# Four banks for the turned rows and two for the logits at the end of the attention layers a1 and a2

## The chip, the cores and the metric

The kernel runs on one core of one Trainium2 chip. The metric is the device time of one execution in microseconds. Three runs of the kernel before were timed, and their median is the number that the change is measured by. Beside them one execution was profiled; all rows below come from it.

## The reference

The reference is a stack of four pairs of layers over x, of 8 batches x 256 tokens x 256 features, with a context of 77 keys per batch:

```python
x = x + tanh(g_xattn[n]) * Ln_xattn(_layernorm(x), ctx, ...)   # n = 0..3
x = x + tanh(g_ffn[n])   * Ln_ffn(_layernorm(x), ...)
```

Attention has 16 heads, of width 16 in layers 0 and 3 and of width 64 in layers 1 and 2. Layer 1 normalises queries and keys to unit length and its output once more by a layer norm; layer 2 has a mask. The expert layers begin with a router. What matters here is the start of each expert layer: `_layernorm(x)`, and from it the router's logits, `xn @ Wr + br` (8 columns in layer 1; in layer 2 8 columns for the gate and 96 for the low-rank parts, 104 in all).

## The kernel before, in words

The kernel is one program of eight stages, a0 f0 a1 f1 a2 f2 a3 f3 (a: attention, f: expert layer). Between stages all engines meet at a barrier, and the semaphores are cleared. x, `residual` in the trace, stays in SBUF as 16 tiles of 128 tokens, two tiles to a batch.

Each attention stage is written by `attend` (line 2278). Its work is placed by hand on steps s; each engine goes through the same steps in order, and functions such as `scores_at(s)` and `output_at(s)` say which piece falls on which step. PSUM has 8 banks: banks 0 to 3 take scores, 4 and 5 the turned probabilities, 6 and 7 are spare. All other uses (queries, squares, values, output, and what is described next) go through the two spare banks in turn: `uses` lists them in TensorE's order, `place` numbers them, `spare` gives bank 6 or 7 by the number's parity, and `take_spare` makes TensorE wait until the use two places earlier has been emptied.

The front (`front_part`, line 807) is the start of the following expert layer, and is done within the attention stage. For each batch b:

- `variance(b)` on VectorE (lines 889 to 894): statistics of x after the attention's output has been added
- `power(b)` on GpSimd (L898): the inverse root
- `normalise(b)` on VectorE (L907): two tiles of x into `xn`. In a2 `xn` is a ring of two batches, so that `normalise(b)` waits for turn(b-2); in a1 every batch has its own place (`xn_all`), which the SP queue also stores to HBM
- `add_row(b)` on GpSimd (L920), in a2 only: a row added to x after `normalise(b)`
- `turn(b)` on TensorE (L927): 4 transposes of 128x128 into one bank
- `turned_out(b)` on ScalarE (L933): the bank to `xT`
- `route(b)` on TensorE (L943): `xT` times the router's weights
- `logits_out(b)` on VectorE (L955, and in a2 L958 too): logits (and low-rank parts) out of the bank

In a1 and a2 (`small` is false, it means heads of width 16) the turns stand at the very end: `rows_at(s)` gives batch b at step GROUPS + 2 + b, when scores, values and the last `output` product have been issued. `route` follows one step behind the turn, and `logits_out` one more. On TensorE a step is `turn(b)`, then `route(b-1)`. On VectorE it is, where they fall on the step, `add_output`, `variance`, `normalise`, `logits_out`, in this order. In a2 `normalise(b+2)` falls on the step of `turn(b)` (batches 2 to 7). In a1, where the output is normalised once more (`own`), `variance(7)` falls on the step of turn(3), and `normalise(7)` on that of turn(4); `variance(7)` waits for GpSimd's additions of batch 7 (L2728).

Of the kernel before, what the change touches and what calls it, by code (L numbers as in the profile page):

```python
# [35 lines left out]
GROUPS = HEADS // GROUP  # L36
# [2241 lines left out]
def attend(env, scope, n, t, front):  # L2278
# [3 lines left out]
    nc, dram, psum, x, ident, tg = env["nc"], env["dram"], env["psum"], env["x"], env["ident"], env["tg"]  # L2282
# [3 lines left out]
    small = hd == 16  # L2286
# [5 lines left out]
    GROUPS = NBATCH * STEPS  # L2292
# [45 lines left out]
    if mask == "given":  # L2338
        mask8, mask_cap = sb("mask8", [P, TILES, CTX], U8), sb("mask_cap", [P, TILES, CTX])
        loads += [(mask8[:], dram["mask"])]  # L2340
    sems = {k: env["sem"](f"{name}l_{k}") for k in (
        "loaded", "made", "q_ready", "q_out", "q_done", "sq_ready", "sq_copied", "sq_turned", "sq_out", "q_inverted",
        "scored", "s_free", "chain", "shift", "exped", "probs", "turned", "pt_out", "multiplied", "att_out",
        "y_ready", "y_out", "inv_spread", "inv_out", "topped", "row_added", "gated_row", "wo_in", "stats", "var_done", "rstd_done", "applied", "gained", "added")}
# [11 lines left out]
    def queries_at(s):  # L2356
        b, j = divmod(s + Q_AHEAD, STEPS)
        return (b, j) if b < NBATCH and j < NQ else None

    def squares_at(s):  # L2360
        h = (s + 4) // 2
        return h if own and s % 2 == 0 and 0 <= h < 2 * NBATCH else None

    def scores_at(s):
        return s + 2 if 0 <= s + 2 < GROUPS else None

    def norm_at(s):
        return s + 1 if 0 <= s + 1 < GROUPS else None

    def turn_at(s):  # L2370
        return s if 0 <= s < GROUPS else None

    def values_at(s):
        return s // 2 - 1 if s % 2 == 0 and 0 <= s // 2 - 1 < 2 * NBATCH else None

    def output_at(s):
        return (s - 5) // STEPS if s >= 5 and (s - 5) % STEPS == 0 and (s - 5) // STEPS < NBATCH else None
# [10 lines left out]
    def rows_at(s):  # L2388
        if small:
            return output_at(s - 3)  # L2390
        return s - BEHIND if 0 <= s - BEHIND < NBATCH else None

    def logits_at(s):
        if small:
            return output_at(s - 4)
        return rows_at(s - 1)

    def logits_out_at(s):
        if small:
            return output_at(s - 5)  # L2400
        return rows_at(s - 2)


    uses = []
    for s in range(FIRST, LAST):
        if queries_at(s):
            uses.append(("q", queries_at(s)[0] * NQ + queries_at(s)[1]))
        if squares_at(s) is not None:
            uses += [("square", squares_at(s)), ("square_turned", squares_at(s))]
        if values_at(s) is not None:  # L2410
            uses += [("values", values_at(s) * AV + m) for m in range(AV)]
        if output_at(s) is not None:
            uses.append(("output", output_at(s)))
        if rows_at(s) is not None:
            uses.append(("rows", rows_at(s)))
        if logits_at(s) is not None:
            uses.append(("logits", logits_at(s)))
    place = {use: k for k, use in enumerate(uses)}
    left_by = {"q": sems["q_out"], "square": sems["sq_copied"], "square_turned": sems["sq_out"], "values": sems["att_out"],
# [2 lines left out]
    def spare(kind, k):  # L2422
        return psum[:, 6 + place[kind, k] % 2, :]

    def take_spare(pe, kind, k):
        before = place[kind, k] - 2
        if before >= 0:
            pe.wait_ge(left_by[uses[before][0]], uses[before][1] + 1)
        return spare(kind, k)

    def score_banks(g):
        return psum[:, 2 * (g % 2):2 * (g % 2) + 2, 0:4 * keys].rearrange("p b (h k) -> p b h k", k=keys)


    scores_read = "exped" if own else "s_free" if mask else "shift"
# [5 lines left out]
    with nc.Block() as block:  # L2441
# [9 lines left out]
        def _(pe):  # L2451
# [28 lines left out]
            def scores(g):  # L2480
                b, hf, tile = group(g)
                rows = slice(tile * P, (tile + 1) * P)
                if rope:
                    pe.wait_ge(sems["q_done"], b + 1)
                else:
                    pe.wait_ge(sems["q_out"], b * NQ + min(NQ, (hf + 1) * max(1, NQ // 2)))
                if g >= 2:
                    pe.wait_ge(sems[scores_read], g - 1)
                if small:
                    for j in range(2):  # L2490
                        part = slice(64 * j, 64 * j + 64)
                        last = nc.tensor.matmul(psum[:, 2 * (g % 2) + j, 0:4 * keys], qT[b % 2][part, hf, rows],
                                                keysT[part, hf, b, :, :], start=True, stop=True)
                else:
                    for j in range(CH):
                        c = hf * CH + j
                        for odd in range(2):
                            part = slice(hd * odd, hd * odd + hd)
                            last = nc.tensor.matmul(psum[:, 2 * (g % 2) + odd, j * keys:(j + 1) * keys],
                                                    qT[b % 2][part, c, rows], keysT[part, c, b, :],  # L2500
                                                    start=True, stop=True)
                last.then_inc(sems["scored"], 1)
# [51 lines left out]
            for s in range(FIRST, LAST):  # L2554
                if scores_at(s) is not None:
                    scores(scores_at(s))
                if queries_at(s):
                    queries(*queries_at(s))
                if turn_at(s) is not None:
                    turn(s, 0)  # L2560
                if squares_at(s) is not None:
                    squares(squares_at(s))
                if turn_at(s) is not None:
                    turn(s, 1)
                if squares_at(s) is not None:
                    turn_squares(squares_at(s))
                if values_at(s) is not None:
                    for m in range(AV):
                        weigh_values(values_at(s), m)
                if output_at(s) is not None:  # L2570
                    output(output_at(s))
                if rows_at(s) is not None:
                    front["turn"](pe, rows_at(s), take_spare(pe, "rows", rows_at(s)))
                if logits_at(s) is not None:
                    front["route"](pe, logits_at(s), take_spare(pe, "logits", logits_at(s)))

        @block.scalar
        def _(act):
# [71 lines left out]
            for s in range(FIRST, LAST):  # L2650
                if queries_at(s):
                    queries_out(*queries_at(s))
                if squares_at(s) is not None:
                    squares_out(squares_at(s))
                if turn_at(s) is not None:
                    turned_out(s)
                if values_at(s) is not None:
                    for m in range(AV):
                        values_out(values_at(s), m)
                if scores_at(s) is not None:  # L2660
                    exps(scores_at(s))
                if rows_at(s) is not None:
                    front["turned_out"](act, rows_at(s), spare("rows", rows_at(s)))

        def add_row(pool, b):
            where = slice(b * TPB, (b + 1) * TPB)
# [88 lines left out]
        def _(dve):  # L2755
# [116 lines left out]
            for s in range(FIRST, LAST + 1):  # L2872
                if output_at(s - 1) is not None:
                    add_output(output_at(s - 1))
                if scores_at(s) is not None:
                    soft(scores_at(s))
                if norm_at(s) is not None:
                    norm(norm_at(s))
                if own and output_at(s - 2) is not None:
                    apply_norm(output_at(s - 2))  # L2880
                if output_at(s - 1 - LAG) is not None:
                    b = output_at(s - 1 - LAG)
                    dve.wait_ge(sems["added" if own else "y_out"], b + 1)
                    front["variance"](dve, b)
                if normed_at(s) is not None:
                    front["normalise"](dve, normed_at(s))
                if logits_out_at(s) is not None:
                    front["logits_out"](dve, logits_out_at(s), spare("logits", logits_out_at(s)))
                if values_at(s) is not None and small:
                    values_out(values_at(s))  # L2890
                if squares_at(s) is not None:
                    sum_squares(squares_at(s))
                if rope and queries_at(s) and queries_at(s)[1] == NQ - 1:
                    turn_positions(queries_at(s)[0])
# [120 lines left out]
```

## Time and profile before

| | us |
|---|---|
| median of 3 runs | 1899.26 |
| lowest and highest | 1893.53, 1905.22 |
| the profiled execution | 1904.71 |
| its span, first to last instruction | 1902.9 |
| mean granted clock of TensorE | 0.945 of full |

In the rows, PE is TensorE, DVE is VectorE, ACT is ScalarE, POOL is GpSimd, and L927 is line 927. Times count from the start of the span. The granted clock is given as a share of 2.4 GHz: 1.00 is that, and 0.50 is 1.2 GHz.

### The profile page before, as it was taken

The page shows a single profiled execution, that of the slowest core. Times are in us where ns is not written, and L with a number is a line of the kernel's source. Part 1 is how long each engine was busy: PE and PEld are TensorE (multiplying, and loading weights), DVE is VectorE, ACT ScalarE, POOL GpSimd, SP SyncE. Part 2 cuts the span into 40 slices and gives each one's busy share as a digit, 9 for nine tenths or more (in the row PEclk, how much of TensorE's full clock was granted, in tenths as well). Part 3 has the DMA queues.
Part 4 walks back from the last instruction along what each step waited for, and adds up shares of the span by engine and source line. Part 5 has one row for each costly group of instructions (what it writes and reads, how often), then busy time and mean ns, then how long its engine had stood idle before and what let it go on. Part 6 is the DMA issues. An engine that isn't in the chain of part 4 may idle for free. (4 is left out here: it accounts for less than half of the span.)

```text
span 1902.9 us, 32108 instructions
## 1 busy us (share of the span) xinstructions
PE 1708.5 (90%) x11648; PEld 1415.0 (74%) x11648; DVE 1266.2 (67%) x2324; ACT 944.4 (50%) x1681; POOL 539.8 (28%) x499
## 2 busy tenths in 40 slices
PE   6998799978899998399999979999789889889997
PEld 4666799943577777399999747888679656678996
DVE  5886687636445563788888658767364678865764
ACT  4653466533676762266666325444254245514660
POOL 2231333241133332244444111000200043403426
PEclk8998899998999997599999989999789999989999
DMA  4002587520100000567777420000010010023864
GB/s 115 12 21 67 190 250 254 154 62 23 52 1 12 7 12 17 193 208 231 230 229 226 161 66 35 1 1 1 1 29 1 12 49 18 18 87 125 255 191 133
DMA packets 96389, 178.41 MB, mean 94 GB/s; under 512 B 25968, under 2 KB 60682, under 8 KB 95162
## 3 DMA queue, kind: packets, MB, share of 16 engines
q1 hardware_dynamic: 84072, 144.23, 23.4%
q0 software_dynamic: 11904, 32.52, 5.9%
q8 instruction: 77, 1.26, 0.3%
q14 instruction: 48, 0.39, 0.1%
q10 hardware_dynamic: 288, 0.00, 0.0%
HBM read 149.70 MB, written 27.00 MB: 93 GB/s over the span
## 5 line engine op out<-in xcount | busy, mean ns | idle before, releaser
L1757 POOL DMA_INDIRECT f_block_rows_home<-normed_x,f_token_of_sb x138 | 169.3, 1227 | 274.3 <-PE psum L1824 229.8
L1804 PE MATMUL psum<-f_block_h_sb,f_w1h_home 128*128 128x256 f32 x736 | 215.1, 292 | 20.2 <-DVE f_w1l_home L1997 9.5
L1804 PE MATMUL psum<-f_block_l_sb,f_w1h_home 128*128 128x256 f32 x736 | 211.0, 287 | 0.0
L1804 PE MATMUL psum<-f_block_h_sb,f_w1l_home 128*128 128x256 f32 x736 | 210.9, 287 | 0.0
L2458 PE MATMUL psum<-a_xT_home,context_w 128*128 128x256 f32 x704 | 180.8, 402 | 16.9 <-PEq L123 13.3
L1814 PE MATMUL psum<-f_w2h_home,f_hidden_h_home 128*128 128x256 f32 x644 | 187.7, 291 | 1.8 <-DVE f_result_sb L1665 0.9
L1814 PE MATMUL psum<-f_w2l_home,f_hidden_h_home 128*128 128x256 f32 x644 | 182.1, 283 | 0.0
L1814 PE MATMUL psum<-f_w2h_home,f_hidden_l_home 128*128 128x256 f32 x644 | 182.0, 283 | 0.0
L2458 PEld LDWEIGHTS psum<-a_xT_home,context_w 128*128 128x128 f32 x704 | 131.3, 196 | 48.0 <-issue 23.1
L2623 ACT ACTIVATE a_probsT_sb<-psum 77x1024 f32<-77x1024 f32 (+1 forms) x128 | 130.8, 1022 | 68.8 <-PE psum L2510 66.2
L1804 PEld LDWEIGHTS psum<-f_block_h_sb,f_w1h_home 128*128 128x128 f32 x736 | 143.9, 195 | 28.3 <-issue 18.4
L1905 ACT ACTIVATE f_hidden_sb<-psum,f_b_sb 128x256 f32<-128x256 f32 x276 | 115.5, 470 | 73.5 <-PE psum L1804 73.3
L2510 PE MATMUL psum<-identity,a_probs_sb 128*77 128x128 f32 (+1 forms) x1024 | 141.5, 280 | 11.0 <-DVE a_inv_sb L2798 8.9
L2510 PEld LDWEIGHTS psum<-identity,a_probs_sb 128*77 128x77 f32 (+1 forms) x1024 | 115.6, 142 | 46.3 <-DVE a_inv_sb L2798 19.7
L2550 PE MATMUL psum<-a_wo_sb,a_attT_sb 128*128 128x256 f32 x640 | 146.8, 385 | 2.6 <-ACT a_attT_sb L2645 1.4
L1804 PEld LDWEIGHTS psum<-f_block_l_sb,f_w1h_home 128*128 128x128 f32 x736 | 144.0, 196 | 0.0
L1804 PEld LDWEIGHTS psum<-f_block_h_sb,f_w1l_home 128*128 128x128 f32 x736 | 143.8, 195 | 0.0
L2550 PEld LDWEIGHTS psum<-a_wo_sb,a_attT_sb 128*128 128x128 f32 x640 | 121.3, 194 | 19.9 <-ACT a_attT_sb L2645 2.7
L1997 DVE TENSOR_TENSOR f_w1l_home<-f_w_sb,f_w1h_home 128x1024 fp32r<-128x1024 f32 x92 | 112.4, 1222 | 29.5 <-ACT f_w1h_home L1926 24.7
L1814 PEld LDWEIGHTS psum<-f_w2h_home,f_hidden_h_home 128*128 128x128 f32 x644 | 123.4, 192 | 2.5 <-DVE f_hidden_l_home L1997 2.5
L1814 PEld LDWEIGHTS psum<-f_w2l_home,f_hidden_h_home 128*128 128x128 f32 x644 | 123.6, 192 | 0.0
L1814 PEld LDWEIGHTS psum<-f_w2h_home,f_hidden_l_home 128*128 128x128 f32 x644 | 123.3, 192 | 0.0
(318 smaller groups left out, 3815.2 us busy)
## 6 DMA issues: line engine op xcount, KB each, us to landing
f_w_sb<-in_f_w SPq DMA_DIRECT2D x161, 512.0 KB, 4.8
sorted_y<-f_result_sb SPq DMA_DIRECT2D x46, 256.0 KB
normed_x<-f_xn_all SPq DMA_DIRECT2D x24, 256.0 KB, 2.1
f_b_row_sb<-in_f_b SPq DMA_DIRECT2D x46, 128.0 KB, 3.6
f_w_sb<-in_f_w SPq DMA_DIRECT2D x23, 256.0 KB, 4.9
f_w_sb<-slots SPq DMA_DIRECT2D x16, 256.0 KB, 6.3
f_block_rows_home<-normed_x,f_token_of_sb POOLq DMA_INDIRECT x138, 4.0
residual<-in_x SPq DMA_DIRECT2D x8, 256.0 KB, 6.3
```

Of the source, the lines that this page charges most:

```text
L1757: nc.gpsimd.indirect_dma_start(block_rows[b % 2][:, h, :], None, xs, bass.IndirectOffsetOnAxis(ap=column, axis=0)).then_inc(sems[f"rows_in ...
L1804: last = nc.tensor.matmul(hid_ps(q)[:, m, :], w, rhs, start=(j == 0), stop=(j == len(parts) - 1))
L1814: last = nc.tensor.matmul(y_ps[h], v, w, start=(begin and j == 0), stop=(end and j == len(parts) - 1))
L1905: nc.scalar.activation(hidden[q][:, m, :], hid_ps(q)[:, m, :], func, bias=bias[:, 0, m:m + 1]).then_inc(sems["hidden_out"], 1)
L1997: nc.vector.tensor_tensor(out[:], whole[:], part[:].bitcast(F32), ALU.subtract).then_inc(sems[sem], 1)
L2458: last = nc.tensor.matmul(bank[:, s * SEQ:(s + 1) * SEQ], w[:, k, c * P:(c + 1) * P], xT[:, k, b * SEQ:(b + 1) * SEQ], start=(k == 0), sto ...
L2510: last = nc.tensor.transpose(psum[0:keys, 4 + part, h * P:(h + 1) * P], probs[g % 2][:, 4 * part + h, :], ident[:])
L2550: last = nc.tensor.matmul(bank[:, tile * D:(tile + 1) * D], attT[:, c, tile * P:(tile + 1) * P], wo[:, c, :], start=(c == 0), stop=(c == N ...
L2623: nc.scalar.activation(probsT[h % 2][:, :, tile * P:(tile + 1) * P].rearrange("p (a h) k -> p a h k", a=2), psum[0:keys, 4:6, :].rearrange ...
```

## The change

Where `small` is false, the turned rows go to the four banks 0 to 3 that the scores have left, in turn, and the logits to the two banks 4 and 5 that the turned probabilities have left. Both leave the list of uses of the spare banks. The first turn waits until all scores have been read, the first route until all turned probabilities have been copied out; from then on each waits for its own bank (four back for rows, two back for logits). `route` now follows two steps behind the turn in place of one, and `logits_out` three in place of two. Where `small` is true (a0 and a3) nothing changes. It applies to a1 and to a2.

```diff
@@ def logits_at / logits_out_at
-        return rows_at(s - 1)
+        return rows_at(s - 2)
...
-        return rows_at(s - 2)
+        return rows_at(s - 3)
@@ uses
-        if rows_at(s) is not None:
+        if small and rows_at(s) is not None:
             uses.append(("rows", rows_at(s)))
-        if logits_at(s) is not None:
+        if small and logits_at(s) is not None:
             uses.append(("logits", logits_at(s)))
@@ new
+    def rows_bank(b):
+        return spare("rows", b) if small else psum[:, b % 4, :]
+
+    def logits_bank(b):
+        return spare("logits", b) if small else psum[:, 4 + b % 2, :]
+
+    def take_rows_bank(pe, b):
+        if small:
+            return take_spare(pe, "rows", b)
+        if b == 0:
+            pe.wait_ge(sems[scores_read], GROUPS)
+        if b >= 4:
+            pe.wait_ge(front["turned_left"], b - 3)
+        return rows_bank(b)
+
+    def take_logits_bank(pe, b):
+        if small:
+            return take_spare(pe, "logits", b)
+        if b == 0:
+            pe.wait_ge(sems["pt_out"], GROUPS)
+        if b >= 2:
+            pe.wait_ge(front["logits_left"], b - 1)
+        return logits_bank(b)
@@ TensorE
-                    front["turn"](pe, rows_at(s), take_spare(pe, "rows", rows_at(s)))
+                    front["turn"](pe, rows_at(s), take_rows_bank(pe, rows_at(s)))
                 if logits_at(s) is not None:
-                    front["route"](pe, logits_at(s), take_spare(pe, "logits", logits_at(s)))
+                    front["route"](pe, logits_at(s), take_logits_bank(pe, logits_at(s)))
@@ ScalarE
-                    front["turned_out"](act, rows_at(s), spare("rows", rows_at(s)))
+                    front["turned_out"](act, rows_at(s), rows_bank(rows_at(s)))
@@ VectorE
-                    front["logits_out"](dve, logits_out_at(s), spare("logits", logits_out_at(s)))
+                    front["logits_out"](dve, logits_out_at(s), logits_bank(logits_out_at(s)))
```

## Rows read from the trace of the kernel before

**Rows 1.** The page's first part: busy time of TensorE, share, instructions.
```profile
PE 1708.5 (90%) x11648; PEld 1415.0 (74%) x11648; DVE 1266.2 (67%) x2324; ACT 944.4 (50%) x1681; POOL 539.8 (28%) x499
```

**Rows 2.** Timeline, TensorE, end of a1: start, length, instruction, count, [idle before <-releaser].
```profile
747.14 1.88 PE L943 MATMUL psum<-f_wr,f_xT_home 128*128 128x8 f32 x8 [1.98 <-DVE f_logits L955]
748.87 1.09 PE L927 MATMUL psum<-identity,f_xn_all 128*128 128x128 f32 x4
749.76 1.71 PE L943 MATMUL psum<-f_wr,f_xT_home 128*128 128x8 f32 x8
...
757.12 3.42 PE L943 MATMUL psum<-f_wr,f_xT_home 128*128 128x8 f32 x16
```

**Rows 3.** Timeline, VectorE, end of a1.
```profile
742.97 0.17 DVE L955 TENSOR_TENSOR f_logits<-psum,f_rb 128x16 f32<-128x16 f32 x1
745.77 0.75 DVE L889 BATCH_NORM_STATS2 stats<-residual 128x6 f32<-128x256 f32 x2 [2.63 <-POOL residual L2728]
...
746.92 0.17 DVE L955 TENSOR_TENSOR f_logits<-psum,f_rb 128x16 f32<-128x16 f32 x1
747.84 0.73 DVE L907 TENSOR_SCALAR f_xn_all<-residual,mv,rstd 128x256 f32<-128x256 f32 x2 [0.75 <-POOL rstd L898]
```

**Rows 4.** Timeline, TensorE, end of a2.
```profile
1341.89 8.64 PE L2550 MATMUL psum<-a_wo_sb,a_attT_sb 128*128 128x256 f32 x32 [0.70 <-ACT a_attT_sb L2645]
...
1351.38 0.66 PE L927 MATMUL psum<-identity,f_xn 128*128 128x128 f32 x4 [0.41 <-DVE residual L2835]
1351.88 1.04 PE L943 MATMUL psum<-f_wr,f_xT_home 128*128 128x104 f32 x8
1353.40 0.63 PE L927 MATMUL psum<-identity,f_xn 128*128 128x128 f32 x4 [0.48 <-DVE f_xn L907]
1357.81 1.38 PE L943 MATMUL psum<-f_wr,f_xT_home 128*128 128x104 f32 x8 [3.78 <-DVE f_low_rank L958]
...
1361.29 2.03 PE L943 MATMUL psum<-f_wr,f_xT_home 128*128 128x104 f32 x8 [1.25 <-DVE f_low_rank L958]
...
1365.42 2.04 PE L943 MATMUL psum<-f_wr,f_xT_home 128*128 128x104 f32 x8 [1.25 <-DVE f_low_rank L958]
...
1372.25 1.92 PE L943 MATMUL psum<-f_wr,f_xT_home 128*128 128x104 f32 x8
...
1374.81 2.34 PE L943 MATMUL psum<-f_wr,f_xT_home 128*128 128x104 f32 x16
```

**Rows 5.** Timeline, VectorE, end of a2 (the second is one tile of the first).
```profile
1352.51 4.89 DVE L907 TENSOR_SCALAR f_xn<-residual,mv,rstd 128x256 f32<-128x256 f32 x6
...
1353.49 1.38 DVE L907 TENSOR_SCALAR f_xn<-residual,mv,rstd 128x256 f32<-128x256 f32 x1
...
1357.33 0.16 DVE L955 TENSOR_TENSOR f_logits<-psum,f_rb 128x16 f32<-128x16 f32 x1
...
1360.15 0.74 DVE L907 TENSOR_SCALAR f_xn<-residual,mv,rstd 128x256 f32<-128x256 f32 x2 [2.40 <-PE psum L927]
...
1377.29 0.35 DVE L958 COPY f_low_rank<-psum 128x192 f32<-128x192 f32 x1
```

**Rows 6.** Timeline, GpSimd, end of a2.
```profile
1353.45 6.30 POOL L920 TENSOR_TENSOR residual<-residual,context_w 128x512 f32<-128x512 f32 x5
```

**Rows 7.** Windows: stretch, length, busy time by engine, granted clock, DMA share, GB/s.
```profile
744.20:760.60 16.40, 14.37 (x69) 13.87 (x68) 2.88 (x14) 2.98 (x5) 2.17 (x3) 0.50 0.05 17
1350.30:1358.50 8.20, 3.52 (x28) 2.83 (x26) 7.08 (x14) 1.79 (x3) 5.82 (x6) 1.00 0.00 0
1358.60:1375.50 16.90, 13.15 (x60) 11.79 (x58) 4.13 (x16) 2.83 (x5) 4.94 (x4) 0.50 0.00 1
1375.70:1379.00 3.30, 1.46 (x13) 1.28 (x12) 1.04 (x5) 0.30 (x1) 0.00 (x0) 1.00 0.00 0
1391.40:1396.10 4.70, 4.70 (x13) 3.72 (x12) 4.09 (x5) 4.28 (x6) 0.00 (x0) 0.50 0.00 0
1396.20:1400.00 3.80, 3.80 (x18) 3.11 (x17) 3.60 (x5) 3.80 (x7) 0.00 (x0) 1.00 0.00 0
```

## The prediction

> **What bounds the kernel now.** I read the page first: TensorE is busy for 90% of the span, no other engine comes near it [rows 1], so what counts is where TensorE stands idle or runs at the lower clock. The change touches only the end of the two attention layers with 64-wide heads: in the code it hangs on `small`, which is false for a1 and for a2 alike, so "second layer" in its name notwithstanding both layers get it. I therefore read two stretches, engine by engine in order of time: 739 to 762 us (end of a1) and 1350 to 1379 us (end of a2). At the end of each stands a barrier of all engines, so whatever ends a front later or earlier moves all that follows by as much.
>
> In a1 [rows 2, 3] TensorE turns batches 0 to 3 and routes 0 and 1, and at 745.17 stands still for 1.98 us: route(2) wants a bank that VectorE's `logits_out`(1) has yet to empty, and VectorE sits in `variance`(7), which waits for GpSimd. `logits_out`(1) runs at 746.92, route(2) at 747.14. From there TensorE runs without a gap to 760.5, at the lower clock. In that run a turn takes 0.89 us to the start of what follows (748.87 to 749.76) and two routes 3.42 with the tail, 1.6 to 1.7 each.
>
> In a2 [rows 4, 5] each kind of work holds the other up. With two banks for everything, route(1) takes the bank of logits(0), so it waits for `logits_out`(0); VectorE has `logits_out`(0) behind `normalise`(4) in its program, and starts it at 1357.33. TensorE is idle for 3.78 us there. Then three routes follow (the first and second stand in the rows, 4.13 us apart), each after a gap of 1.25 us, since route(b) waits for `logits_out`(b-1), that stands behind `normalise`(b+3), and that waits for turn(b+1), which stands behind route(b-1). Only when the normalisations are over do the routes follow without gaps, 2.56 us apart (1372.25 to 1374.81). The last copy of VectorE starts at 1377.29 and takes 0.35.
>
> **The change part by part.** It adds no instruction and takes none away: 8 turns (4 transposes each), 8 routes (8 products each, as the trace counts them) and their copies out in each layer, and the same DMAs. Earlier uses of banks 6 and 7 stand ahead of all rows and logits in the list, so their places stay. The new waits at b = 0 (scores read, probabilities copied out) are long met when the last `output` product ends, so I cost them at nothing; the cover is the whole of that product, 8.6 us in a2 [rows 4].
>
> *a1.* Turns 0 to 3 and routes 0 and 1 lose their bank waits, and turn(4) now stands ahead of route(2). But `logits_out`(0) moves one step later on VectorE, from before `variance`(7) to behind it: it now starts where `logits_out`(1) did, at 746.92 [rows 3], and route(2) needs just that one (bank 4 again). So route(2) stays at 747.14, with turn(4) already behind it. `logits_out`(1) follows `normalise`(7), ready at about 748.6; route(3) comes after route(2) and turn(5), at 747.14 + 1.6 + 0.9 = 749.6, so that wait is met with 1 us in hand. What remains from 747.14 is six routes and three turns in place of six and four: the gain is one turn at the lower clock, **0.9 us**.
>
> *a2, first part.* turn(1) no longer waits 0.41 us for `output`(7), which brings nothing: turn(2) still waits for `normalise`(2), and stays at 1353.40 [rows 4]. route(0) moves behind it, 1353.9 to 1354.8. turn(3) follows `normalise`(3) at 1355.1, route(1) follows that and needs no emptied bank now (before: 1357.81), turn(4) follows `normalise`(4), which ends at 1357.4, at 1357.65.
>
> *a2, VectorE.* A normalisation costs 0.37 us per tile alone (0.74 for two) and 1.38 us a tile where GpSimd's `add_row` runs beside it, one operation of 1.26 us after another from 1353.45 to 1359.75 [rows 5, 6]. Before, `normalise`(5) came at 1360.15, after that series; now turn(3) releases it early and it runs inside, 1357.33 to about 1360.0: two contended tiles, 2.7 us in place of 0.74. Only then comes `logits_out`(0), at 1360.0, and ends at 1360.4; route(2), which needs bank 4 again, starts at about 1360.7. This is the one large wait that is left (2.5 us). `normalise`(6) then runs 1360.4 to 1362.1 (one tile against `add_row`(5)), `logits_out`(1) to 1362.6, `normalise`(7) to 1364.3 by the same count, `logits_out`(2) to 1364.7.
>
> *a2, the end.* From 1360.7 TensorE has six routes and three turns to do. A route takes 0.87 us at the full clock (the 1.04 us block less its 0.17 tail) and 1.7 to 1.8 at the lower; a turn 0.5 and 0.86 to 0.89 [rows 2, 4]. Lower clock throughout: 6 x 1.71 + 3 x 0.87 = 12.9, ending 1373.6, VectorE at 1374.2, against 1377.63: gain **3.4**. Full clock throughout: 6 x 0.87 + 3 x 0.5 = 6.7, plus about 1.4 of waits, for route(3) needs `logits_out`(1) (1362.6) and route(4) `logits_out`(2) (1364.7): end 1368.9, VectorE 1369.4, gain **8.2**. In between: before, the clock fell at about 1358.5, after the 3.78 us of idle time and one route, and came back at about 1375.6, 4.2 us after the gaps had ceased at 1371.4 [rows 7]. The changed kernel is idle in much the same place, from 1358.2 to 1360.7, so I let it fall too; but it has no gaps from 1360.7 on, so I let it return between 1365.4 and 1368.8. That gives ends of 1370.2 and 1371.8, gains of 7.4 and 5.8; I take the middle, **6.6**.
>
> A page speaks against that return. The Trainium skill (TensorE: Matmul & The Clock Gate, section "A second HAM failure mode: psum-queue depth-cycling") says that a kernel cycling through PSUM banks can leave TensorE such small gaps between groups that its clock swings down again, and the change spreads this work over six banks. By that page the sum for a2 would be the 3.4 of the lower clock. The trace leaves both open: in a1 TensorE was without gaps for 13 us and stayed at the lower clock, in a2 it came back after 4 [rows 7]. I go by a2's own rows, which are of the same instructions.
>
> **The sum.** 0.9 + 6.6 = 7.5 us. Against the profiled execution that is 1904.71 - 7.5 = 1897.2 (its span 1902.9 and 1.8 around it). That execution lies 5.4 above the median of the runs, 1899.26; the forecast goes by the median: 1899.26 - 7.5 = **1891.8**.
>
> **The rivals.**
> - *The lower clock stays through a2's front.* For it: a1's long stretch, and the 17 us at half in a2 before [rows 7]. Against it: the return at 1375.6. Gain 0.9 + 3.4 = 4.3: 1895.0. The page above says this one.
> - *The clock never falls in a2.* For it: route(1) now stands in the middle of the old 3.78 us gap. Against it: 2.5 us without work just after. Gain 0.9 + 8.2 = 9.1: 1890.2.
> - *A wait takes the place of the one removed in a2*, and the change does not do what it says there: if turns ran so far ahead that VectorE and GpSimd block each other in every batch, all of `normalise`(5) to (7) at 2.7 us, `logits_out` behind each, the batches go at 2.7 + 0.4 + about 1 and keep their old 4.1 us. Against it: `add_row` b waits for `normalise` b, so the series runs dry. Only a1's 0.9 would be left: 1898.4.
> - *Slower than before.* The lower clock goes on into f2's first products: 13 instructions of PE in 4.70 us at half there [rows 7], about 0.36 us each, where the full clock would need some 0.2, so 0.4 to 0.5 us is lost for each us that it lasts longer. It decides from 7.5 / 0.45 = 17 us longer; at 25 us the time is 1899.26 - 7.5 + 11.3 = 1903.1. For it: a1's long stretch. Against it: before, the clock was back at 1396.2, 5 us after the first of these products, and the profile has no cause for a longer stretch.
>
> **How the numbers follow.** Return of the clock within the front 0.45, lower throughout 0.2, never falls 0.2, a wait in its place 0.1, slower 0.05. The mechanism alone spans 1890.2 to 1898.4. The three runs of before spread over 11.7 us, so a median of three has some 4 us either way of its own; and each of the few falls and rises of the clock behind the change can move. That gives **1883 to 1901**. A measurement of this kernel can tell about 1% (19 us) from no change, and no case here comes near it: faster by over 1% 0.03, within 1% 0.95, slower 0.02.
>
> **What would show it.** In a2: no 3.78 us gap ahead of the second route; `normalise`(5) with tiles of 1.35 us; `logits_out`(0) at about 7.5 us after `variance`(7) ended; VectorE's last copy 3.4 to 8.2 us nearer to the end of the last `output` product than its 27 us before. In a1: five turns ahead of route(2), which still starts right behind VectorE's `variance`(7) and `logits_out`(0), and the front shorter by about 0.9 us. The prediction is wrong if `logits_out`(0) in a2 comes much later than that, if a1's front grows (VectorE's `logits_out`(1) behind a late `normalise`(7)), or if the saving in the fronts is there and the whole does not show it.

## The result, and the profile after

| | before | changed |
|---|---|---|
| median of 20 runs, us | 1902.82 | 1893.64 |
| lowest and highest | 1893.53, 1912.1 | 1884.44, 1898.02 |
| span of the profiled execution | 1902.9 | 1891.6 |

The ratio is 0.9948, 95% interval 0.9935 to 0.9962: 9.9 us faster (7.2 to 12.4), within 1%. The forecast was 7.5 us and 1891.8. Over 20 runs the median of before is 1902.82 and not the 1899.26 of the first three, so the difference is what to compare.

I call "front" the time from the end of the 32 instructions of the stage's last `output` product (L2550, in the changed kernel L2574) to the end of VectorE's last copy out of the logits banks; 1.2 us of barrier follow in both kernels. a1's front went from 21.2 to 20.5 us, a2's from 27.1 to 19.9.

The end of a2 on TensorE, in order of time (start, length, instruction, count, idle before and its releaser), answers to [rows 4]:

```profile
1340.92 7.17 PE L2574 MATMUL psum<-a_wo_sb,a_attT_sb 128*128 128x256 f32 x32 [0.70 <-ACT a_attT_sb L2669]
1347.93 1.04 PE L927 MATMUL psum<-identity,f_xn 128*128 128x128 f32 x8
1350.86 0.66 PE L927 MATMUL psum<-identity,f_xn 128*128 128x128 f32 x4 [1.89 <-DVE f_xn L907]
1351.35 1.04 PE L943 MATMUL psum<-f_wr,f_xT_home 128*128 128x104 f32 x8
1352.48 0.66 PE L927 MATMUL psum<-identity,f_xn 128*128 128x128 f32 x4
1352.97 1.04 PE L943 MATMUL psum<-f_wr,f_xT_home 128*128 128x104 f32 x8
1355.12 0.63 PE L927 MATMUL psum<-identity,f_xn 128*128 128x128 f32 x4 [1.11 <-DVE f_xn L907]
1357.92 2.04 PE L943 MATMUL psum<-f_wr,f_xT_home 128*128 128x104 f32 x8 [2.16 <-DVE f_low_rank L958]
1359.75 1.06 PE L927 MATMUL psum<-identity,f_xn 128*128 128x128 f32 x4
...
1364.70 2.82 PE L943 MATMUL psum<-f_wr,f_xT_home 128*128 128x104 f32 x24
```

The gap of 3.78 us ahead of route(1) and the three of 1.25 us are gone. One of 2.16 us is left, ahead of route(2), released by L958: the copy of logits(0). VectorE in the same stretch ([rows 5]), then GpSimd ([rows 6]):

```profile
1352.35 5.17 DVE L907 TENSOR_SCALAR f_xn<-residual,mv,rstd 128x256 f32<-128x256 f32 x4
1357.44 0.16 DVE L955 TENSOR_TENSOR f_logits<-psum,f_rb 128x16 f32<-128x16 f32 x1
1357.52 0.34 DVE L958 COPY f_low_rank<-psum 128x192 f32<-128x192 f32 x1
1357.79 1.55 DVE L907 TENSOR_SCALAR f_xn<-residual,mv,rstd 128x256 f32<-128x256 f32 x2
...
1367.65 0.35 DVE L958 COPY f_low_rank<-psum 128x192 f32<-128x192 f32 x1
```
```profile
1351.01 6.36 POOL L920 TENSOR_TENSOR residual<-residual,context_w 128x512 f32<-128x512 f32 x5
```

Four tiles take 5.17 us beside `add_row`, `normalise`(5) among them, and `logits_out`(0) stands behind it. The windows (length, busy time of PE, PEld, DVE, ACT and POOL, granted clock, DMA) answer to [rows 7]:

```profile
1348.10:1356.70 8.60, 4.56 (x36) 3.77 (x34) 8.46 (x14) 2.88 (x5) 6.46 (x6) 1.00 0.00 0
1356.90:1363.60 6.70, 5.68 (x27) 5.68 (x28) 4.30 (x13) 0.83 (x2) 4.28 (x4) 0.50 0.01 2
1363.80:1367.80 4.00, 3.72 (x34) 3.55 (x33) 1.56 (x8) 0.76 (x2) 0.00 (x0) 1.00 0.00 0
```

The clock fell in the gap and came back inside the front, 5.8 us after the gap ended. In a1 ([rows 2, 3]):

```profile
740.42 1.47 PE L927 MATMUL psum<-identity,f_xn_all 128*128 128x128 f32 x12
741.80 1.03 PE L943 MATMUL psum<-f_wr,f_xT_home 128*128 128x8 f32 x8
...
748.22 1.87 PE L943 MATMUL psum<-f_wr,f_xT_home 128*128 128x8 f32 x8 [3.62 <-DVE f_logits L955]
```
```profile
746.84 0.75 DVE L889 BATCH_NORM_STATS2 stats<-residual 128x6 f32<-128x256 f32 x2 [2.72 <-POOL residual L2752]
...
747.99 0.17 DVE L955 TENSOR_TENSOR f_logits<-psum,f_rb 128x16 f32<-128x16 f32 x1
748.90 0.73 DVE L907 TENSOR_SCALAR f_xn_all<-residual,mv,rstd 128x256 f32<-128x256 f32 x2 [0.74 <-POOL rstd L898]
```

The one gap before route(2) has grown from 1.98 to 3.62 us: all work that can be done ahead is done, and `logits_out`(0) now waits behind `variance`(7).

Of the 11.3 us between the two spans the fronts are 7.9. Another 3.0 are the two last `output` products, the same 32 instructions in both kernels: 8.64 in a2 before, 7.17 after, and 8.68 and 7.17 in a1. That is the clock's doing and not the change's: before, it stood at 0.50 over the first 3 us of both, and in the changed kernel at 1.00 throughout; over the thirteen profiles of this study a1's product takes 7.17 to 10.23 us. A front is therefore a better measure of one change here than a span.

### The profile page after: what moved, and what is told of

The parts are those of the page before. It is cut to its first block and busy times, and to the rows that moved or that the text cites. A ratio compares the mean times of both kernels' runs of the same rounds, so it can differ in the third digit from the quotient of the medians.

```text
span 1891.6 us, 32100 instructions
## 1 busy us (share of the span) xinstructions
PE 1699.2 (90%) x11648; PEld 1407.9 (74%) x11648; DVE 1267.4 (67%) x2324; ACT 942.5 (50%) x1681; POOL 544.6 (29%) x499
## 5 line engine op out<-in xcount | busy, mean ns | idle before, releaser
L2482 PE MATMUL psum<-a_xT_home,context_w 128*128 128x256 f32 x704 | 180.4, 401 | 17.5 <-PEq L123 13.3
L2574 PE MATMUL psum<-a_wo_sb,a_attT_sb 128*128 128x256 f32 x640 | 144.5, 381 | 2.6 <-ACT a_attT_sb L2669 1.4
L2574 PEld LDWEIGHTS psum<-a_wo_sb,a_attT_sb 128*128 128x128 f32 x640 | 119.7, 191 | 19.0 <-ACT a_attT_sb L2669 2.3
```

What stands on the lines that cost most here:

```text
L2482: last = nc.tensor.matmul(bank[:, s * SEQ:(s + 1) * SEQ], w[:, k, c * P:(c + 1) * P], xT[:, k, b * SEQ:(b + 1) * SEQ], start=(k == 0), sto ...
L2574: last = nc.tensor.matmul(bank[:, tile * D:(tile + 1) * D], attT[:, c, tile * P:(tile + 1) * P], wo[:, c, :], start=(c == 0), stop=(c == N ...
```

## The experiments

All numbers of a front are from the one profiled execution of each kernel; "gain" for the whole is from the ratio with its interval, against the runs of before on the same chip. a1's front repeats well where a1's instructions are the same: 21.2 in two profiles (before, a2 alone), 20.5 in five (changed, a1 alone, add_row held, no add_row, filled gap). a2's moves more, with the clock: 27.1 and 27.6, 19.9 and 19.2. In the row "add_row held" GpSimd ends last, and a2's front is counted to GpSimd's end.

| kernel | a1's front | a2's front | fronts together, gain | whole, gain |
|---|---|---|---|---|
| before | 21.2 | 27.1 | | |
| changed | 20.5 | 19.9 | 7.9 | 9.9 (7.2 to 12.4) |
| a2 alone | 21.2 | 19.2 | 7.9 | 4.2 (0.4 to 7.8) |
| a1 alone | 20.5 | 27.6 | 0.3 | -1.9 (-6.1 to 2.3) |
| banks only | 18.8 | 19.0 | 10.6 | 11.0 (7.4 to 14.6) |
| lag only | 22.5 | 26.2 | -0.3 | 0.6 (-2.9 to 4.2) |
| logits first | 18.0 | 17.0 | 13.3 | 12.0 (8.8 to 15.2) |
| add_row held | 20.5 | 18.3 | 9.5 | 10.7 (6.9 to 14.5) |
| no add_row | 20.5 | 13.5 | 14.3 | 15.8 (12.6 to 19.2) |
| filled gap | 20.5 | 18.2 | 9.7 | 11.2 (8.2 to 14.5) |
| four logit banks | 16.4 | 18.1 | 13.8 | 16.9 (12.7 to 21.3) |
| rows added early | 16.3 | 14.8 | 17.3 | 19.6 (15.4 to 23.8) |
| wide products in a1 | 14.1 | 14.8 | 19.5 | 19.6 (13.3 to 25.7) |

**One layer at a time.** In the first kernel a1 takes its banks from the list as before, in the second a2 does:

```diff
+    shared = small or own          # a2 alone; "small or (not own)" for a1 alone
-        if small and rows_at(s) is not None:
+        if shared and rows_at(s) is not None:
...
-        return rows_at(s - 2)
+        return rows_at(s - (own and 1 or 2))
```

> The change in a2 alone; a1 is as before. Theory A (the gain is a2's gaps; a1 gives only one turn at the lower clock): a2's front, from the end of the last output product to VectorE's last copy, takes 18.5 to 21 us as in the changed kernel (19.7; before 27.1), a1's front 21.2 as before; the whole 6 to 9 us under before, ratio about 0.996. Rival B (a1 carries a good part of the 9 us, as the title says 'second layer'): the whole only 2 to 5 us under before.

> The change in a1 alone; a2 is as before. Theory A: a1's front 20.3 to 20.6 us in place of 21.2, route(2) right behind variance(7) and logits_out(0), a2's front 27 us; the whole 0.5 to 1 us under before, which these runs cannot tell from nothing. Rival B: the whole 4 us or more under before.

Measured: 0.9978 (0.9959 to 0.9998) and 1.001 (0.9988 to 1.0032). The fronts fall exactly where theory A put them: a2's 19.2 with a1's at 21.2, then a1's 20.5 with a2's at 27.6. So by the fronts a2 carries 7 to 8 us and a1 0.7, and rival B falls; a1 alone gains at most 2.3 us in the whole, where B wanted 4 or more. The whole times of a2 alone fit less well: the ratio gives 4.2 us where its front gained 7.9, just outside its interval and inside the 2 to 5 that stood for rival B, though its median (1895.02 against 1902.45) is 7.4 lower. The two ratios together give 2.3 of the change's 9.9 us, the two medians 7.9. I go by the fronts, which show where the time went; why the ratios fall short is open.

**Banks or lag.** The change has two parts. Banks only puts `logits_at` and `logits_out_at` back to s - 1 and s - 2; lag only is the kernel before with s - 2 and s - 3:

```diff
-        return rows_at(s - 2)      # banks only, from the changed kernel
+        return rows_at(s - 1)
...
-        return rows_at(s - 3)
+        return rows_at(s - 2)
```

> Six banks, but route again one step behind the turn and logits_out two, in both layers. Theory C (the banks give all of the gain, the longer lag only puts logits_out behind later work of VectorE): in a1 logits_out(0) is back ahead of variance(7), route(2) runs in the gap and route(3) is the one that waits, so that five routes and three turns are left behind it and a1's front takes 18.7 to 19.1 us (changed kernel 20.5); in a2 logits_out(0) comes before normalise(5), and the front takes 18.5 to 20.5 us. The whole 8 to 11 us under before. Rival D (the lag is what frees the engines from each other): a2's front goes back to 24 us or more, and the whole is within 4 us of before.

> The longer lag alone, with the two spare banks of before. Theory C: in a1 route(1) now waits for logits_out(0) behind variance(7), one route more is left behind it, and the front takes 22.5 to 23.2 us; in a2 route(1) waits for logits_out(0) behind normalise(5), gaps of about 1.2 us follow, and the front takes 27 to 30 us. The whole 1 to 4 us over before. Rival D: a2's front at 23 us or less, the whole 4 us or more under before.

Measured: 0.9942 (0.9923 to 0.9961) for the banks, 0.9997 (0.9978 to 1.0015) for the lag. Banks only, TensorE in a1 and VectorE beside it:

```profile
743.60 0.63 PE L927 MATMUL psum<-identity,f_xn_all 128*128 128x128 f32 x4
746.55 1.88 PE L943 MATMUL psum<-f_wr,f_xT_home 128*128 128x8 f32 x8 [2.32 <-DVE f_logits L955]
...
754.08 3.42 PE L943 MATMUL psum<-f_wr,f_xT_home 128*128 128x8 f32 x16
```
```profile
742.38 0.17 DVE L955 TENSOR_TENSOR f_logits<-psum,f_rb 128x16 f32<-128x16 f32 x1
745.19 0.75 DVE L889 BATCH_NORM_STATS2 stats<-residual 128x6 f32<-128x256 f32 x2 [2.64 <-POOL residual L2752]
```

`logits_out`(0) is back ahead of `variance`(7) (742.38), and it is route(3) that waits: one route less behind the gap, 1.7 us less front than in the changed kernel. The lag alone, in a2:

```profile
1357.28 2.03 PE L943 MATMUL psum<-f_wr,f_xT_home 128*128 128x104 f32 x8 [4.71 <-DVE f_low_rank L958]
1359.11 1.06 PE L927 MATMUL psum<-identity,f_xn 128*128 128x128 f32 x4
1361.41 2.03 PE L943 MATMUL psum<-f_wr,f_xT_home 128*128 128x104 f32 x8 [1.25 <-DVE f_low_rank L958]
```

The old gap is longer (4.71 in place of 3.78), and gaps of 1.25 us are still there. Its a2 front of 26.2 is 0.9 better than before and under the 27 expected, and the whole is not the 1 to 4 us slower that was expected but the same within its interval: there are two of these gaps in place of three, and the clock came back in time for the last three routes. Theory C stands for a1 in full: the banks gain 2.4 us there, the lag takes 1.7 back. In a2 the banks gain 8.1 without the lag and 7.2 with it; the difference of 0.9 is about what the clock moves a front from run to run (0.7, 19.2 and 19.9 for the same instructions), so one profile of each does not tell it from nothing. Rival D falls. No run splits the banks further, into the four for the rows and the two for the logits.

**Where logits_out stands.** VectorE does `logits_out` at the start of its step, not at the end:

```diff
+                if not small and logits_out_at(s) is not None:
+                    front["logits_out"](dve, logits_out_at(s), logits_bank(logits_out_at(s)))
                 if output_at(s - 1) is not None:
                     add_output(output_at(s - 1))
...
-                if logits_out_at(s) is not None:
+                if small and logits_out_at(s) is not None:
```

> The changed kernel, but VectorE does logits_out at the start of its step, ahead of add_output, variance and normalise. Theory E (what is left of the gaps is logits_out waiting behind other work in VectorE's program): in a1 logits_out(0) starts near 743 in place of behind variance(7), route(2) runs in the gap, and the front takes 17.5 to 18.5 us (changed kernel 20.5); in a2 route(2) starts right behind turn(4), 2 us earlier, and the front takes 17.5 to 19.2 us (changed kernel 19.7). The whole 10 to 13 us under before. Rival F (normalise is the limit, not where logits_out stands): a2's front stays at 19.5 us or over and only a1's part is gained, 8 to 10 us under before in all.

Measured: 0.9937 (0.992 to 0.9954), fronts 18.0 and 17.0. In a2 route(2) follows turn(4) with no gap, and the clock did not fall in the front, which is why it is a little better than expected:

```profile
1354.76 0.63 PE L927 MATMUL psum<-identity,f_xn 128*128 128x128 f32 x4 [1.05 <-DVE f_xn L907]
1355.22 1.04 PE L943 MATMUL psum<-f_wr,f_xT_home 128*128 128x104 f32 x8
1356.58 0.63 PE L927 MATMUL psum<-identity,f_xn 128*128 128x128 f32 x4 [0.33 <-DVE f_xn L907]
```

What releases TensorE there is now L907, `normalise`, and no longer a bank. In a1 route(2) runs in the old gap, as expected, and route(3) is the one that still waits for a bank, 2.32 us. Theory E stands.

**VectorE beside GpSimd.** Two kernels: in the first GpSimd begins a2's eight `add_row` only after `normalise`(7); the second leaves them out.

```diff
                 for b in range(NBATCH):
                     front["power"](pool, b)
+                front["all_normed"](pool)    # held: pool.wait_ge(sems["normed"], NBATCH)
                 for b in range(NBATCH):
                     front["add_row"](pool, b)             # left out in the second kernel
```

> The changed kernel, but in a2 GpSimd begins its eight add_row only when normalise(7) is done. Theory F (the tiles of normalise take 1.35 us because add_row runs beside them): all tiles of normalise(2) to (7) take 0.4 us, normalise(7) ends some 7 us after variance(7) in place of 11, TensorE is done 5 us earlier and at the full clock; but the eight add_row then take 10.2 us in a row and end the front, at 18.5 to 19.5 us. The whole 0 to 1 us under the changed kernel. Rival (something else slows those tiles): they still take 1.35 us, and the front grows to 23 us or more.

> The changed kernel without a2's eight add_row, so that the row is not added to x (that part of the computation is left out): it prices them. Theory F: tiles of normalise at 0.4 us throughout, a2's front 13 to 14.5 us in place of 19.7, the whole 5 to 7 us under the changed kernel, 14 to 17 under before. Rival G (TensorE and its clock are the limit of a2's front, not VectorE beside GpSimd): a2's front at 17 us or more.

Measured: 0.9944 (0.9924 to 0.9964) and 0.9917 (0.9899 to 0.9934). With `add_row` held, VectorE and GpSimd in a2:

```profile
1342.18 0.74 DVE L907 TENSOR_SCALAR f_xn<-residual,mv,rstd 128x256 f32<-128x256 f32 x2 [0.18 <-PE psum L930]
1343.49 0.73 DVE L907 TENSOR_SCALAR f_xn<-residual,mv,rstd 128x256 f32<-128x256 f32 x2 [0.57 <-PE psum L930]
...
1358.18 0.28 DVE L1055 TENSOR_REDUCE f_m_sb<-f_logits 128x16 f32<-128x128 f32 x1 [6.03 <-PEq L123]
```
```profile
1347.12 9.83 POOL L920 TENSOR_TENSOR residual<-residual,context_w 128x512 f32<-128x512 f32 x8 [5.41 <-DVE f_xn L907]
```

Two tiles take 0.74 us, everywhere. VectorE's last copy ends 13.5 us behind the output product, and GpSimd's series ends at 18.3 and sets the end. Without the series the front is 13.5: the same tiles run beside nothing, so the eight operations cost 19.9 - 13.5 = 6.4 us as the changed kernel places them (some of it through the clock, which stays at 1.00 here). The page of the Trainium skill "SBUF — State Buffer", section "SBUF: two separate sides", describes a pair of ports that VectorE and GpSimd share as an exclusive lock: for some kinds of VectorE's instructions, the engine that starts first holds it for the whole instruction and the other stands still. VectorE's side agrees: a tile takes 0.37 us alone and 1.35 beside an `add_row` of 1.27, and the four tiles in 5.17 us end at 1357.52, 0.15 us behind the end of the series at 1357.37, as if each tile had to wait for an `add_row` to be over. GpSimd's side shows no such wait: five take 6.36 us beside the tiles, 1.27 each, where eight take 9.83 alone, 1.23 each. The profile does not show the lock itself.

**The clock in a2's gap.** Four products whose results nobody reads, ahead of route(2):

```diff
+                if logits_at(s) == 2 and not small and not own:
+                    pe.wait_ge(sems["y_out"], NBATCH)
+                    for _ in range(4):
+                        nc.tensor.matmul(psum[:, 6, 0:D], attT[:, 0, 0:P], wo[:, 0, :], start=True, stop=True)
```

> The changed kernel with 4 products of 256 columns, whose results nobody reads, put ahead of route(2) in a2, where TensorE otherwise stands idle for 2.2 us. Theory H (the clock falls because of the idle time around route(2), and costs 1.5 us): the granted clock stays at 1.00 through a2's front, which takes 17.8 to 18.8 us in place of 19.7. Rival (the fall has another cause, or the products come too late): the clock falls all the same, and the front takes 19.5 us or more.

Measured: 0.9941 (0.9924 to 0.9957), front 18.2:

```profile
1346.50:1350.90 4.40, 2.41 (x21) 2.00 (x19) 4.29 (x11) 1.68 (x3) 2.28 (x3) 1.00 0.00 0
1351.10:1354.30 3.20, 3.20 (x16) 2.99 (x15) 3.20 (x3) 0.60 (x1) 3.20 (x3) 0.50 0.00 0
1354.60:1364.60 10.00, 9.10 (x68) 7.90 (x67) 7.33 (x22) 2.39 (x4) 4.97 (x4) 1.00 0.01 2
```

The front's length is as theory H has it, the clock is not: it fell for a short stretch ahead of the added products, 1.8 us after TensorE had stood idle for 1.90 us waiting for `normalise`(2), and was back when they ran. The changed kernel has the same wait there (1.89 us) and kept its clock behind it, so the cause of this fall is open. From route(2) to the end it stayed at 1.00, and that part took 8.3 us against 10.1 in the changed kernel. Whether the products kept it there, this one profile doesn't tell.

**Four banks for the logits.** From the kernel with logits first, with the short lag of before and the two spare banks as well:

```diff
-        return spare("logits", b) if small else psum[:, 4 + b % 2, :]
+        return spare("logits", b) if small else psum[:, 4 + b % 4, :]
...
-        if b >= 2:
-            pe.wait_ge(front["logits_left"], b - 1)
+        if b == 2:
+            pe.wait_ge(sems["y_out"], NBATCH)
+        if b >= 4:
+            pe.wait_ge(front["logits_left"], b - 3)
```

> As the run with logits_out at the start of VectorE's step, but with the short lag of before (route one step behind the turn, logits_out two) and four banks for the logits, the two spare ones being the third and fourth. Theory E (in a1 the only thing that held TensorE back is the emptied logits bank): routes 0 to 5 and turns 0 to 6 are done before variance(7) is, one route, one turn and one route are left behind it, and a1's front takes 11.5 to 13.5 us in place of 20.5; in a2 no route waits for a bank, normalise(7) ends at 13 to 13.6 us as before and sets the end, and the front takes 15.5 to 16.7 us. The whole 18 to 21 us under before, ratio 0.989 to 0.991. Rival (TensorE's work at the lower clock or ScalarE's copies are the next limit in a1): a1's front stays over 15 us and the whole is less than 16 us under before.

Measured: 0.9911 (0.9888 to 0.9933), a1's front 16.4, a2's 18.1: faster, and still a miss on both fronts. In a1 no route waits for a bank, as expected, but the clock falls in the middle of unbroken work, and TensorE at the lower clock is the limit. The rival was right on the front (over 15 us); the whole, 16.9, is just over the 16 that it allowed and under the 18 of theory E:

```profile
740.43 0.96 PE L943 MATMUL psum<-f_wr,f_xT_home 128*128 128x8 f32 x8
741.24 0.94 PE L927 MATMUL psum<-identity,f_xn_all 128*128 128x128 f32 x4
741.97 1.71 PE L943 MATMUL psum<-f_wr,f_xT_home 128*128 128x8 f32 x8
743.54 1.09 PE L927 MATMUL psum<-identity,f_xn_all 128*128 128x128 f32 x4
```

A route takes 0.96 us and the next one 1.71, with no gap between. In a2 the clock fell as well, for 6.8 us, which is enough to account for the front's miss of its 15.5 to 16.7.

**Rows added early.** The kernel above, and GpSimd does `add_row`(0) and (1) before it waits for `variance`(7):

```diff
-                for b in range(NBATCH):
+                for b in range(NBATCH - 1):
                     front["power"](pool, b)
-                for b in range(NBATCH):
+                for b in range(2):
+                    front["add_row"](pool, b)
+                front["power"](pool, NBATCH - 1)
+                for b in range(2, NBATCH):
                     front["add_row"](pool, b)
```

> The run before, and in a2 GpSimd does add_row(0) and add_row(1), whose batches have been normalised long before, ahead of its wait for variance(7), under the last output product where VectorE is idle. Theory F (normalise's tiles of 1.35 us are the time beside add_row): the series that runs beside normalise is two operations (2.5 us) shorter, normalise(7) ends at 11 to 12.3 us, and a2's front takes 13.5 to 15 us; the whole 1 to 2.5 us under the run before. Rival: the tiles are slowed as often as before and the front is within 0.5 us of the run before.

Measured: 0.9897 (0.9875 to 0.9919), a2's front 14.8. Windows of a1 (two) and a2:

```profile
738.90:743.70 4.80, 4.46 (x42) 4.25 (x40) 3.29 (x12) 2.28 (x4) 2.06 (x2) 1.00 0.16 55
743.90:755.00 11.10, 10.92 (x54) 10.83 (x52) 2.73 (x13) 2.39 (x4) 1.82 (x2) 0.50 0.08 25
1342.30:1357.00 14.70, 12.00 (x96) 10.66 (x94) 13.03 (x34) 4.67 (x8) 8.39 (x7) 1.00 0.01 1
```

`normalise`(7) ends 11.6 us behind the output product in place of 13.1, as theory F has it. The front gained 3.4; I put 1.5 to the contention and the rest to the clock, which stayed at 1.00 in a2. The whole times of this kernel and the one before can't be told apart. In a1 TensorE is busy for 10.92 of 11.10 us, at 0.50.

**Wide products in a1.** The kernel above, and in a1 one product of 256 columns ahead of each turn from the third on, into the bank that the turn then overwrites:

```diff
+                    bank = take_rows_bank(pe, rows_at(s))
+                    if own and rows_at(s) >= 2:
+                        nc.tensor.matmul(bank[:, 0:D], attT[:, 0, 0:P], wo[:, 0, :], start=True, stop=True)
+                    front["turn"](pe, rows_at(s), bank)
```

> The run before (rows added early), and in a1 one product of 256 columns, whose result nobody reads, ahead of each turn from the third on: six products more in a1. Theory K (in a1 TensorE works without a gap and is yet set back to the lower clock, because its front has only transposes and products of 8 columns): the clock stays at 1.00 to the end of a1's front, a turn, a route and the added product together take some 1.8 us in place of 2.46, and the front takes 12.5 to 14.5 us in place of 16.3; the whole up to 3 us under the run before. Rival L (the clock falls in a1's front whatever it does there): the clock is at 0.50 from 4 to 6 us behind the last output product on, the added products take 0.8 us each, and the front takes 18 us or more; the whole 2 to 5 us over the run before.

Measured: 0.9897 (0.9865 to 0.993), a1's front 14.1 in place of 16.3:

```profile
736.70:750.70 14.00, 13.42 (x108) 12.47 (x106) 6.13 (x25) 4.67 (x8) 4.05 (x4) 1.00 0.12 39
```
```profile
743.20 0.96 PE L943 MATMUL psum<-f_wr,f_xT_home 128*128 128x8 f32 x8
744.01 0.68 PE L2601 MATMUL psum<-a_wo_sb,a_attT_sb 128*128 128x256 f32 x2
744.53 0.60 PE L927 MATMUL psum<-identity,f_xn_all 128*128 128x128 f32 x4
744.97 0.96 PE L943 MATMUL psum<-f_wr,f_xT_home 128*128 128x8 f32 x8
```

TensorE does more work, and the front is shorter: the clock stays at 1.00 to its end, and a batch takes 1.77 us with the added product where it took 2.46 without. Theory K stands, by one profile: in each of the other twelve the clock fell within a1's front. The runs' mean granted clock points the same way (0.955 to 0.961 in all six here, 0.951 to 0.956 in the five of the kernel before). In the whole the 2.2 us can't be told from the run before.

## Why the prediction was right

**a1, 0.9 us: measured 0.7.** This step held: route(2) starts 7.6 us behind the output product in both kernels, with five turns ahead of it in place of four, and `logits_out`(0) stands where `logits_out`(1) stood. What I did not see is that the lag itself costs there: I took the later `logits_out`(0) as given, where banks only shows that it throws away 1.7 us.

**a2, first part.** turn(2), route(0), turn(3), route(1), turn(4) came in this order, released as worked out; `logits_out`(0) starts 7.3 us behind the end of `variance`(7), where I had 7.4.

**a2, VectorE.** `normalise`(5) runs inside `add_row`'s series at 1.35 us a tile, and route(2) is the wait that is left, 2.16 us for the forecast 2.5. Holding and leaving out `add_row` confirmed the cause. From turn(4) to the end route(2)'s wait is the only one of TensorE, so the rival of a wait in every batch falls. `normalise`(6) went 1.55 us for two tiles, and `normalise`(7) ended 13.6 us behind the output product, 13.8 forecast.

**a2, the end: 6.6 forecast, 7.2 measured.** The likeliest case is the one that came: the clock fell at the gap and returned in the front. One reading behind it was wrong. The prediction has the gaps of the kernel before end at 1371.4 and the clock return 4.2 us later; the last gap ended at 1369.57:

```profile
1369.57 2.04 PE L943 MATMUL psum<-f_wr,f_xT_home 128*128 128x104 f32 x8 [1.25 <-DVE f_low_rank L958]
```

The return came 6.0 us behind it, and 5.8 us behind the last gap in the changed kernel. The stretch that the prediction allowed, 4.7 to 8.1 us, covers both, so the sum did not suffer.

The rule of the Trainium skill (TensorE: Matmul & The Clock Gate, section "A second HAM failure mode: psum-queue depth-cycling"), that cycling through banks with small gaps lets the clock swing, was the ground for a clock that stays low and for 3.4 us. Here the clock fell and came back over six banks. In other kernels it did not fall in a2's front at all: with six banks and gaps up to 1.90 us (logits first) and with eight and gaps up to 0.45 us (rows added early); with eight and gaps up to 1.11 us (four logit banks) it fell for 6.8 us. So these runs bear out that it can swing, and do not show that the number of banks decides it. The rival of the lower clock falls, as does the one that it never falls, for this execution at least: the fronts of 19.2 and 19.9 for the same a2 instructions show that it varies, and which of these cases a run meets is in part luck.

**The rest of the 9.9 us.** The fronts give 7.9, the interval begins at 7.2, so nothing need be added. No stage behind the fronts took the gain back: f2's first product (L1379) starts 13.8 us behind the end of VectorE's last copy in both. The slower rival (the lower clock going on into f2) did not come: the clock was back 2.4 us after f2's first product, before it was 4.7.

```profile
1370.60:1384.00 13.40, 5.98 (x21) 4.62 (x22) 12.59 (x20) 8.56 (x13) 0.00 (x0) 0.50 0.29 88
1384.30:1388.00 3.70, 3.70 (x17) 3.02 (x17) 3.70 (x4) 3.70 (x5) 0.00 (x0) 1.00 0.00 0
```

It remains open whether that belongs to the change or to how the clock happened to fall; what is shown is the fronts. That the median came out only 1.8 us from the forecast is luck in part: it starts from a median of before that was 3.6 us too low, and the medians then fell by 9.2 us and not 7.5.

## What to carry to other kernels

When a bank is wanted back, look at what stands ahead of its emptying in the emptying engine's program: more banks paid 10.6 us here, a longer lag in the schedule paid nothing and cost 1.7 where it moved the emptying behind a wait for a third engine. Put short copies out of PSUM at the start of a step, and give otherwise idle banks to the work that is left at the end of a stage. Where many small stages end at a barrier, time the stage from a fixed instruction in the trace; the span moves by more than the change does.

## What the runs showed of the hardware that I had not expected

TensorE's clock fell in the midst of unbroken work: in the kernel with rows added early TensorE was busy for 10.92 of 11.10 us and at 0.50, doing transposes and products of 8 columns; in the one with four logit banks it fell likewise. With one product of 256 columns more per batch it stayed at 1.00, and the longer list of work was done 2.2 us sooner. The Trainium skill (TensorE: Matmul & The Clock Gate, section "Part 4: PE-mode transpose") says that the full clock doesn't engage for transposes. The trace agrees only in part: transposes were a third of a1's time (0.89 of 2.46 us a batch), but a2's front in the kernel with rows added early has the same transposes beside products of 104 columns, with TensorE busy for 12.00 of 14.70 us, and stayed at 1.00, a turn taking 0.5 us. So the transposes by themselves don't explain the fall, and no run here singles out the products of 8 columns either.
